# A new order of the pipelined steps on all engines in the layers of a two-block transformer kernel

## The reference

```python
def attn_layer(x, Wqkv, qs, ksc, Wo):          # x is shifted by one token in half of its columns
    q, k, v = jnp.split(x @ Wqkv, 3, -1)         # 16 heads of 64
    q, k = l2norm(q) * qs, l2norm(k) * ksc
    q = q * cos * scale + rotate_half(q) * sin * scale
    k = k * cos * inv + rotate_half(k) * sin * inv
    return local_attention(q, k, v) @ Wo         # windows of 32, each sees itself and the one before

def ffn_layer(x, g, bln, W1, b1, W2, b2):       # x is shifted here too
    xn = (x - mu) / jnp.sqrt(var + 1e-05) * g + bln
    a, gate = jnp.split(xn @ W1 + b1, 2, -1)
    return a * gelu(gate) @ W2 + b2

for i in range(6):
    x = attn_layer(shift_tokens(x), ...) + x
    x = ffn_layer(shift_tokens(x), ...) + x
```

## Time and profile before

| | us |
|---|---|
| median of 3 runs | 3810.37 |
| lowest, highest | 3803.43, 3812.31 |
| the profiled execution, its own time | 3809.82 |
| its span in the trace | 3808.0 |
| one cycle in steady state, in turn | 30.87 and 30.95 |

### The profile page before, as it was taken

How to read it: one execution, slowest core, us unless ns; L and a number is a source line. 1 busy time by engine, 2 the same in 40 slices (tenths; PEclk the granted TensorE clock), 3 DMA queues, 4 the chain that set the end, 5 groups by cost and what they waited for, 6 DMA issues and landing times. The chain is left out here.

```text
span 3808.0 us, 161553 instructions
## 1 busy us (share of the span) xinstructions
PE 3516.9 (92%) x67234; PEld 2893.7 (76%) x67234; DVE 2986.5 (78%) x4277; ACT 2686.3 (71%) x4153; POOL 2393.2 (63%) x2866
## 2 busy tenths in 40 slices
PE   5888888599999999999999999999999999999995
PEld 3555555378888888888888888888888888888874
DVE  3455554588888888888888888888888888888874
ACT  2444444377777778877778877888778887887772
POOL 1010000577777777777777777777777777777762
PEclk9999999799999999999999999999999999999997
DMA  1000000132222332222322223222232222322221
GB/s 54 4 3 3 6 3 3 41 89 69 67 70 63 74 90 70 70 66 73 90 66 66 66 72 90 66 66 66 72 89 67 67 71 63 75 71 68 67 66 56
DMA packets 161761, 228.28 MB, mean 60 GB/s; under 512 B 42259, under 2 KB 60633, under 8 KB 161497
## 3 DMA queue, kind: packets, MB, share of 16 engines
q1 hardware_dynamic: 161624, 226.85, 23.8%
HBM read 21.00 MB, written 4.19 MB: 7 GB/s over the span
## 5 line engine op out<-in xcount | busy, mean ns | idle before, releaser
L1109 POOL TENSOR_TENSOR by_cos<-by_cos,by_sin 128x1024 f32<-128x1024 f32 x384 | 921.3, 2399 | 49.2 <-DVE by_sin L1453 49.2
L1115 POOL TENSOR_TENSOR by_cos<-by_cos,norms 128x1024 f32<-128x1024 f32 x384 | 724.0, 1907 | 0.5 <-issue 0.3
L1451 DVE TENSOR_TENSOR by_cos<-proj,turns 128x1024 f32<-128x1024 f32 x384 | 470.0, 1224 | 216.6 <-ACT squares L1344 216.2
L1188 PE MATMUL proj<-qkv_hi,xs_hib 128*128 128x512 f32 x1152 | 523.9, 455 | 57.8 <-DVE by_sin L1453 42.2
L1344 ACT ACTIVATE squares<-proj 128x1024 f32<-128x1024 f32 x384 | 392.5, 1022 | 179.9 <-PE proj L1190 172.6
L1324 ACT ACTIVATE vb<-proj 128x1024 f32<-128x1024 f32 x192 | 195.4, 1017 | 422.7 <-PE proj L1190 401.1
L1453 DVE TENSOR_TENSOR by_sin<-proj,turns 128x1024 f32<-128x1024 f32 x384 | 466.1, 1214 | 0.0
L1457 DVE TENSOR_REDUCE sumsb<-squares 128x16 f32<-128x1024 f32 x384 | 464.0, 1208 | 1.5 <-DVE w_lo L1514 1.5
L1190 PE MATMUL proj<-qkv_hi,xs_lob 128*128 128x512 f32 x1152 | 459.2, 399 | 0.8 <-issue 0.8
L1189 PE MATMUL proj<-qkv_lo,xs_hib 128*128 128x512 f32 x1152 | 458.5, 398 | 0.0
L1197 PE MATMUL ring<-ident,by_cos 128*128 128x128 f32 x3072 | 404.4, 275 | 1.7 <-POOL by_cos L1115 0.8
(11 more groups left out here) (172 smaller groups left out, 8208.7 us busy)
## 6 DMA issues: line engine op xcount, KB each, us to landing
v_win<-vb SPq DMA_DIRECT2D x1152, 128.0 KB, 2.4
v_win<-vb SPq DMA_DIRECT2D x768, 64.0 KB, 2.0
in_qkv<-L_ffn_Wqkv SPq DMA_DIRECT2D x12, 768.0 KB
wo<-L_ffn_Wo SPq DMA_DIRECT2D x6, 512.0 KB, 4.0
x_tok<-L_attn_x SPq DMA_DIRECT2D x8, 256.0 KB, 4.7
residual<-x_tok SPq DMA_DIRECT2D x8, 256.0 KB, 2.0
o_x<-residual SPq DMA_DIRECT2D x1, 2048.0 KB, 7.9
out<-o_x SPq DMA_DIRECT2D x8, 256.0 KB, 2.3
```

Of the source, the lines that this page charges most:

```text
L1109: nc.gpsimd.tensor_tensor(both, both, by_sin[:, j, :], ALU.add).then_inc(e[f"{w_}_added"].sem, 1)
L1115: nc.gpsimd.tensor_tensor(heads, heads, inverse, ALU.mult).then_inc(e[f"{w_}_ready"].sem, 1)
L1188: nc.tensor.matmul(out, xs_hi[:, tile], qkv_hi[:, cols], start=True, stop=False)
L1451: nc.vector.tensor_tensor(of_heads(by_cos[:, t % 2, j, :]), heads, table(0), ALU.mult)
```

## The change

The strings of PE, ACT, DVE and POOL are replaced. Every step of before is there once; the steps and the waits inside them are the same.

```diff
-    "PE": "Tq:0 V:-2 Pq:2 mean Tk:0 X:-1 O:-2 Pk:2 var V:-1 S:0 spread Pv:2 O:-1 Tq:1 Pq:3 Tk:1 W:-1 Pk:3 GG "
-    "S:1 AA X:0 Pv:3 F4",
+    "PE": "Pq:2 mean Tq:0 Tk:0 O:-2 var Pk:2 X:-1 spread S:0 V:-1 Pv:2 Tq:1 O:-1 Pq:3 Tk:1 W:-1 Pk:3 GG S:1 AA "
+    "X:0 Pv:3 F4 V:0",
-    "Act": "XSa:2 XSa:3 EV:1 EQ:0 IG:1 XF EXP:-1 Qq:2 FSQ EK:0 EX:-1 MK:0 EO:-2 Qk:2 EV:2 EO:-1 EQ:1 Qq:3 IG:2 "
-    "MK:1 XH EXP:0 EK:1 Qk:3 GEL EX:0",
+    "Act": "XSa:2 EV:1 XF XSa:3 IG:1 EXP:-1 Qq:2 FSQ EQ:0 EK:0 MK:0 EO:-2 Qk:2 EX:-1 EV:2 EQ:1 EO:-1 IG:2 Qq:3 "
+    "EXP:0 EK:1 XH MK:1 Qk:3 GEL EX:0",
-    "DVE": "R:-2 XC Cq:2 Rq:2 RS:-1 FV Ck:2 R:-1 XM Rk:2 MX:0 SB:0 Cq:3 Rq:3 RS:0 WX:-1 Ck:3 AM Rk:3 XN MX:1 "
-    "SB:1",
-    "Pool": "Mq:0 XSd:2 N:1 Ak:1 Aq:2 FP Mq:1 Mk:1 XSd:3 Ak:2 XL N:2 Aq:3 Mk:2",
+    "DVE": "XC Cq:2 FV Rq:2 RS:-1 XM Ck:2 R:-1 MX:0 Rk:2 SB:0 Cq:3 Rq:3 RS:0 WX:-1 Ck:3 AM Rk:3 MX:1 SB:1 XN R:0",
+    "Pool": "Aq:1 Ak:1 Mq:0 XSd:2 Mk:0 N:1 FP Mk:1 Mq:1 XSd:3 Aq:2 Ak:2 N:2 XL",
```

## The result

The changed kernel is slower. Its median is 3844.16 us of 5 runs (3841.07 to 3848.36), against 3809.26 us of 5 runs of the kernel before (3803.43 to 3812.31). The ratio is 1.0095, with an interval from 1.0081 to 1.0108. The forecast was 3797, in a range up to 3813.

A forecast was written before the change was run, and what follows sets the result against it. PE was taken as the busiest engine, bound by a loop through ACT's key copy `EK:0` and `O:-2`. 80 plain cycles x -0.38 = -30.4, + 11.4 + 5 + 1 = -13.0, from 3809.8 to 3797; range 3777 to 3813.

The forecast's parts named there:

- What else is moved lies beside this: Plain cycle: other moved steps, such as `R:0`, `XN`, `V:0` and POOL's, were taken to lie off the time-setting loop.
- The rival: PE's loop end: `V` right before the jump and `Pq:2` right behind it make the kernel slower, 3845 at 0.6; chance 0.10.
- j: Assumed cost of PE's loop jump behind `V` per cycle; time 3797 + 80 x j, deciding from 0.3 us.
- the sum for the loop: Plain cycle through ACT and PE, `Qk:3` to `Qk:3`: 30.53 in the mean against 30.91, a gain of 0.38.
- the signs that I named: Trace: plain cycles 30.53, `O:-2` 0.9 earlier, DVE idle before `FV`, `Pv:2` barely waiting, `w_lo` at 2 us or more, its cycle 33.9.
- the two that I said would refute it: Trace: a plain cycle at 30.7 or above, or a wait with no releaser before `Pq:2`.
- the term: Cycle with `w_lo` in front of `Ck:2`: 33.9 against 32.00, 1.9 more in each of 6 layers, 11.4, between 2 and 13.
- The last cycle of a layer: DVE sets the time there; `R:0` and `XN` follow later: 1.0 more in each of 5 changes of layer, 5 in all.
- The cycle behind it: Cycle after a layer's last: expected to gain like the plain ones, 0.38.
- ruled by fill and drain: Five more cycles in the run's first and last ones, left out of the 80 that gain.
- the rule that the prediction cited for this: DVE instructions with two SBUF inputs and POOL instructions reading SBUF lock each other out for their whole length.

The follow-up runs named there:

- the first experiment: Changed kernel with `V` first instead of last in PE's string, so the loop's jump stands between `F4` and `V`; 3807.21 us, ratio 0.9989 to the kernel before.
- the kernel with both edits: Changed kernel with PE's jump between `F4` and `V` and `w_lo` on DVE moved behind `Rk:2`; 3781.66 us, ratio 0.9922 to the kernel before.
- the third experiment: Kernel before, same cyclic order on PE, with only its loop's jump moved to behind `V` and in front of `Pq:2`; 3838.89 us, ratio 1.0079.
- the second experiment: Changed kernel with PE's loop jump one step later, behind `Pq` instead of in front of it; 3812.07 us, ratio 1.0006 to the kernel before.

## Why the prediction was wrong

**The step that failed** is the one in "What else is moved lies beside this": `V:0` behind `F4`, "with its input long ready". I asked only whether `V`'s input would be late, and counted the jump that now stands behind it at nothing. It costs 0.44 us in each turn of the loop, and the first experiment gives 0.46 a plain cycle back. The rival had it with this very mechanism, with the slack of `Pq:2` counted as nothing, as it is. With 0.45 for its j it reads 3797 + 80 x 0.45 = 3833, so 36 of the 47 us by which the forecast was off. I gave it 0.10, on the argument that "the loop's jump costs nothing visible in the plain cycles of before". That argument was the mistake: in the kernel before, the jump stood behind `F4`, and it shows no cost there in the changed order either. A price seen in one place was taken for the price of the thing. The range ended at 3813, although the text named 3845.

**What held.** Without the jump the sum for the loop is right nearly row by row: `O:-2` at 12.87 (forecast 12.97), `Pv:2` at 19.86 (19.93 and 19.89), from there to `Qk:3` 10.6 (10.64), the cycle 30.46 (30.53). Of the signs that I named, DVE's wait before `FV`, `Pv:2` without a wait and `w_lo` above 2 us are there; so are the two that I said would refute it, a plain cycle above 30.7 (30.92) and a wait with no releaser before `Pq:2`.

**Terms mis-sized.** `w_lo`: its wait was right (2.81 against 2.7), and the term was +11.4 against +21.9. Five of the six cycles grew by 4.0 each, from 32.0 to 36.0, and the first by 2.0. What was missing in the five is 1.6 us in each for PE's work at half clock, and 0.5 for the jump, which the forecast's cycle of 30.53 lacks. I had read the granted clock only where it was 1.00 and had no term for a wait that makes the work behind it slower. The last cycle of a layer: +2.0 each instead of +1.0. The first experiment takes only 0.1 of this away, so the jump is not in it; its part is POOL's scaling beside the turns (3.57 against 1.75, partly given back by `qkv_lo`, 1.93 against 2.98), and DVE's later arrival at `Rk:3`: in the first experiment's trace `qkv_lo` starts 27.0 behind `XC`, before 25.7. The cycle behind it was forecast to gain 0.4 and lost 1.3, at a clock of 0.96. With the turns ahead of `Cq`, as against the kernel with both edits, it keeps its length (32.15 against 32.22) although 1.6 us of turns now stand in it.

**A gain I had not seen.** The last four cycles took 10.1 us less, and the prediction put them at nothing, "ruled by fill and drain". PE is out of its loop there. In these four cycles of the kernel before, PE has eight waits that nothing released, 10.7 us in all, at `V`, at `S` and once in a projection; in the changed kernel it has three, 4.6 us in all. The longest stands in front of the first `V` behind the loop:

```profile
3669.08 1.00 PE L1237 MATMUL ring<-v_win,pTb 64*32 64x64 f32 x74 [2.47 <-issue]
```

That cycle took 35.23 us before and 30.53 in the changed kernel. It took 30.89 in the third experiment, which has PE's order of before and the jump behind `V`: for this part, then, it is again the place where the loop ends that counts. For the other waits no experiment parts the order from the place.

A smaller part is PE's clock while the pipeline drains. The sixteen matmuls of the last output projection, in the kernel before, in the changed one, and in that with `w_lo` moved back, whose PE order is the changed kernel's:

```profile
3749.30:3755.90 6.60, 6.58 (x17) 5.34 (x18) 0.00 (x0) 1.51 (x2) 0.72 (x1) 0.55 0.01 2
```
```profile
3784.20:3788.00 3.80, 3.69 (x18) 3.31 (x19) 0.00 (x0) 1.74 (x2) 0.73 (x1) 1.00 0.02 4
```
```profile
3771.90:3777.40 5.50, 5.45 (x18) 4.56 (x19) 0.00 (x0) 1.68 (x2) 0.72 (x1) 0.67 0.01 3
```

The last cycle was 20.3 us in the changed kernel and 24.4 in the other, with the same rows in the same order. So up to 4 us of this gain belong to the one execution and not to the change.

**Not settled.** Why `V` ahead of the jump, 128 small matmuls with a weight load each, makes it cost 0.37 to 0.44 us and six large ones next to nothing is not shown; nor do the runs part the jump from the register instructions at the turn of the loop. The Trainium skill, "Runtime: NRT & Kernel Launch", section "Instruction fetch mechanics", says that a taken branch breaks the sequential prefetch of instructions, and that it stalls the engine until the target is fetched if the target lies outside the two pages of instructions held. The body of this loop is the same wherever the jump stands, so by that rule alone every place of it should pay or none. The runs show that it is paid only where the work right ahead of it is small pieces, which would fit a stall hidden behind large matmuls, but no run here looks into the fetch itself. Open too is why the clock falls behind one wait and not behind another of the same length.

## What to carry over

Where a loop is rolled up, the place of its jump is part of the order: look at what stands right ahead of it, and try it behind a few large instructions before an order is judged; here that alone was worth 0.8 to 1.1%. A wait of PE is not over when it ends: read the granted clock of the stretch behind it, and give the work that may follow at half speed a term of its own; behind waits of 2.7 us and more it was 1.5 to 2.6 us here, in most cases and not in all. And where an operation of DVE with two inputs in SBUF is placed by hand, its price is what POOL does at that moment, 0.4 us or 2, so it belongs beside POOL's small operations.

## What the runs showed of the hardware that I had not expected

- PE's loop jump: 0.44 us behind `V` (128 small matmuls, each with its weight load), in both orders; nothing that shows behind `F4`, and with the jump behind the six large matmuls of `Pq` the cycle was 0.05 longer than with it behind `F4`.
- The granted clock: it went to 0.50 for 3 to 6 us, and eight transposes took 1.9 us instead of 1.04. Behind waits of PE of 3.8 us and more in the layers it did so every time, behind 2.42 in all five cases of the kernel with POOL's old order, behind 2.70 to 2.71 in five of five in the changed kernel, four of five in the second experiment and none of four in the one with the mean behind the jump, behind 3.02 in three of five. Behind 2.02 it stayed at 1.00 with half of `w_lo` (five of five) and in four of five in the kernel before. Waits of 1.77 and 2.90 with 0.69 of work between them brought it down in all five. So the length of the wait alone does not decide.
- DVE and POOL: half of `w_lo` took 2.13 us beside POOL's scaling and its other half 0.55; a pair of turns 0.81 or 2.7. The long ones end 0.3 to 0.9 us behind the end of POOL's scaling in the rows looked at (`w_lo` in the changed kernel 0.8), which agrees with the rule that the prediction cited for this.
- In the drain the same instructions took 3.69 or 5.45 us, as the clock happened to stand.
